# First layer of a two-layer network: VectorE makes the scaled input of the next tile between the driving term and the scan of this one

## The reference, cut to what matters

```python
Bm = sequence @ W_B.T + b_B
Cm = sequence @ W_C.T + b_C
Delta = softplus(sequence @ W_Delta.T + b_Delta + bias_Delta)
A_bar = exp(A * Delta[..., None])
B_bar = 1.0 / A * (A_bar - 1.0) * Bm[..., None, :]
...
state = state * Ab + x[..., None] * Bb      # one step of the scan over tokens
y = einsum('bdn,bn->bd', state, c)
...
x = layernorm(x + scan_layer(x))
x = layernorm(x + experts(x))               # silu(gate) * up, down, weighted by the router
```

## Time and profile before

| | |
|---|---|
| median of 3 runs | 3291.12 us |
| the profiled execution, its own time | 3293.81 us |
| its span (first to last instruction) | 3291.9 us |
| granted TensorE clock, mean | 0.97 |
| PE, busy share of the span | 91% |
| DVE | 80% |
| ACT | 68% |
| POOL | 68% |

### The profile page before, as it was taken

How to read it: one execution, slowest core, us unless ns; L and a number is a source line. 1 busy time by engine, 2 the same in 40 slices (tenths; PEclk the granted TensorE clock), 3 DMA queues, 4 the chain that set the end, 5 groups by cost and what they waited for, 6 DMA issues and landing times. The chain is left out here.

```text
span 3291.9 us, 40141 instructions
## 1 busy us (share of the span) xinstructions
PE 2997.8 (91%) x11488; PEld 1708.8 (52%) x11488; DVE 2647.5 (80%) x3505; ACT 2227.9 (68%) x3409; POOL 2244.2 (68%) x1623
## 2 busy tenths in 40 slices
PE   3589999999999999999889999999988899999998
PEld 1146666666666676778434434434434444444443
DVE  5989989898989899555799999999999545555553
ACT  2357676676767666666575666666665688888887
POOL 3478888888878788777477767777786444444444
PEclk7689999999999999999999999999999999999999
DMA  3024445444444444445222222222222333333332
GB/s 99 13 86 132 128 124 134 124 122 133 125 123 135 119 124 124 136 145 161 87 70 72 74 71 71 74 70 72 91 70 67 91 102 98 104 106 104 106 108 82
DMA packets 214983, 335.49 MB, mean 102 GB/s; under 512 B 36739, under 2 KB 72740, under 8 KB 214380
## 3 DMA queue, kind: packets, MB, share of 16 engines
q1 hardware_dynamic: 214764, 332.93, 35.3%
HBM read 325.69 MB, written 7.09 MB: 101 GB/s over the span
## 5 line engine op out<-in xcount | busy, mean ns | idle before, releaser
L1702 POOL TENSOR_TENSOR c_hc<-c_h,c_c_rep 128x1024 f32<-128x1024 f32 x256 | 604.2, 2361 | 251.4 <-DVE c_h L1746 183.0
L1746 DVE TENSOR_TENSOR_SCAN c_h<-c_decay,c_carry,c_v_ps 128x512 f32<-128x512 f32 x512 | 654.6, 1351 | 1.3 <-issue 1.3
L2170 ACT ACTIVATE d_hmid<-d_up,n_b 128x1024 f32<-128x1024 f32 x512 | 532.2, 1119 | 89.4 <-PE d_up L2072 89.2
L1581 ACT ACTIVATE c_decay<-c_dt,c_a_cols 128x512 f32<-128x512 f32 x512 | 363.9, 722 | 334.3 <-DVE c_h L1746 332.8
L2210 POOL TENSOR_TENSOR d_acc<-d_acc,d_prod 128x512 f32<-128x512 f32 x240 | 310.1, 1311 | 394.4 <-DVE d_prod L2278 394.4
L1398 PE MATMUL c_y_ps<-c_hc,ident 128*128 128x512 f32 x1024 | 500.7, 612 | 46.6 <-POOL c_hc L1702 37.5
L687 POOL TENSOR_TENSOR ab_inner_low<-ab_inner,ab_inner_high 128x512 fp32r<-128x512 f32 x264 | 341.8, 1295 | 241.5 <-ACT ab_inner_high L570 240.2
L559 ACT ACTIVATE ab_gate_ps<-ab_gate_ps,ab_raw_d 128x512 f32<-128x512 f32 x264 | 174.6, 661 | 430.0 <-PE ab_gate_ps L414 429.9
L669 POOL TENSOR_TENSOR ab_hc<-ab_h,ab_c_rep 128x512 f32<-128x512 f32 x256 | 331.7, 1296 | 86.7 <-DVE ab_h L740 65.1
L1736 DVE TENSOR_TENSOR c_v_ps<-c_dtu,c_b_ps 128x512 f32<-128x512 f32 x512 | 346.6, 766 | 1.7 <-PE c_b_ps L1389 1.1
L675 POOL TENSOR_TENSOR ab_gu_low<-ab_raw_gu,ab_gu_high 128x512 fp32r<-128x512 f32 x264 | 341.3, 1293 | 4.4 <-ACT ab_gu_high L546 4.4
(11 more groups left out here) (312 smaller groups left out, 6412.0 us busy)
## 6 DMA issues: line engine op xcount, KB each, us to landing
ab_raw_gu<-in_b_experts SPq DMA_DIRECT2D x264, 256.0 KB, 3.4
ab_w_rep<-ab_w_scratch SPq DMA_DIRECT2D x264, 256.0 KB, 3.6
c_c_rep<-c_c_scratch SPq DMA_DIRECT2D x256, 256.0 KB, 3.1
d_w_rep<-d_w_scratch SPq DMA_DIRECT2D x1024, 64.0 KB, 2.1
ab_raw_d<-in_b_experts SPq DMA_DIRECT2D x264, 129.0 KB, 2.1
ab_raw_x<-in_xT SPq DMA_DIRECT2D x32, 256.0 KB, 4.8
out<-xT SPq DMA_DIRECT2D x8, 512.0 KB, 3.0
xT<-in_xT SPq DMA_DIRECT2D x1, 3072.0 KB, 13.2
```

What stands on the lines that cost most here:

```text
L1581: nc.scalar.activation(decay[:, i % DEC, :], dt[:, s, m, :], ACT.Exp, scale=a_cols[:, n * NM + m:n * NM + m + 1]).then_inc(decay_ready, 1)
L1702: nc.gpsimd.tensor_tensor(hc[:, q % HC], h[:, q % HR], c_rep[:, q % BC].unsqueeze(1).broadcast_to([P, PAIR, CH]), ALU.mult).then_inc(hc_re ...
L1746: nc.vector.tensor_tensor_scan(out=h[:, q % HR, m, :], data0=decay[:, i % DEC, :], data1=v_ps[m][:], initial=carry[:, i:i + 1], op0=ALU.mu ...
L2170: nc.scalar.activation(hmid[:, (2 * q + r) % HM], up_ps[(2 * q + r + c * 2 * NU) % UP][:], ACT.Gelu, bias=b1[:, e:e + 1]).then_inc(gelu_re ...
```

## The change

The VectorE program of the first layer is written in another order. Inside a step the driving term of tile n comes first, then the scaled input of tile n + 1, then the scan of tile n. The scaled input of tile 0 of a chunk is made before the loop (first chunk) or at the end of step 32 of the iteration before. No instruction is added or removed, and no wait is added: each instruction keeps its own semaphore waits. Orders of all other engines are as before.

```diff
                     tile = n < NT and below(i, NCH)
                     if tile:
-                        scaled_input(i, s, n)
                         driving(i, n)
+                        if n + 1 < NT:
+                            scaled_input(i, s, n + 1)
                         scan(i, n)
                     if valid(g):
                         gated_input(g)
                         gate_times_up(i, n, g)
                         weigh(i, n, g)
+                    if n == NT and below(i, NCH - 1):
+                        scaled_input(i + 1, 1 - s, 0)
...
             dve.sem_inc(carry_ready, NT // NQ)
+            scaled_input(0, 0, 0)
             over_chunks(dve, NCH, lambda c, s, first, last: iteration(c, s))
```

## The result

The changed kernel takes 3306.88 us (median of 4 runs, 3305.0 to 3307.59); the kernel before, measured beside it, 3291.10 (4 runs, 3288.63 to 3291.36). The ratio is 1.0047, with a 95% interval of 1.0034 to 1.0060: slower by 15.8 us, where +4 was forecast. That is inside the range of 3282 to 3309, but outside the 3286 to 3302 of the forecast's own case. The execution that was profiled took 3305.0 us, its span is 3303.1; the profiled execution of before had 3293.81 and 3291.9.

What follows compares the result with a forecast made beforehand. With experts TensorE bounds the kernel, able to give back at most 8.1 of 180.5 us a stretch; without experts VectorE does. +2 with experts and +2 without, on 3291.1, made 3295 us; range 3282 to 3309.

Steps and rivals of the forecast that it cites:

- the forecast's own case: Whole kernel: the pairs of VectorE instructions close, handed back as waits for the replication; 3286 to 3302 us, chance 0.54.
- What an instruction costs by where it stands: VectorE: with independent successors the driving term takes 0.61 and the scaled input 0.65 us, saving 0.26 a tile, 8.2 a stretch.
- The nine waits: With experts, scaled inputs behind late TensorE gates wait for the replication at nine steps of 33, 12.3 us a stretch.
- The sum with experts: Stretch of 33 steps beside experts: 12.3 new waits less 8.2 saved less 3.8 vanished waits, +0.3 us; +2 over 6.3 stretches.
- the waits for the tanh: VectorE with experts: of 9.6 us a stretch spent waiting for ScalarE's tanh, 3.8 go.
- ten steps: Steps with experts counted beside six whole iterations, together 6.3 stretches at +0.3 us each.
- The first stage: The 55 tiles without experts: -0.9 us for regular tiles and +2.7 for late places, about +2.
- The tile at half clock: Without experts, scan end to scan end: 2.82 us at half clock where a tile took 2.71, and 2.52 at full clock.
- the clock's mix: First stage: mean clock 0.64 read as 72% half and 28% full, giving 2.2 - 3.1 = -0.9 us.
- the late places: First stage, replications behind projections and averages: 5.5 us, about half hidden beside VectorE's extra pieces, so +2.7.
- the replication in TensorE's queue decides: Rival: nine waits each 0.2 us longer, or first-stage late places paid fully at half clock; 3299 to 3312, chance 0.23.
- The prediction's bound: With experts, TensorE's unchanged work can give back at most 8.1 of 180.5 us a stretch, however fast VectorE becomes.

Runs made afterwards that it cites:

- experiment 9: The whole change plus three unread TensorE matmuls behind the replication of most tiles without experts, against the kernel before: 3298.99 us, ratio 1.0023.
- experiment 2: New VectorE order only in the 55 tiles without an expert, against the kernel before: 3301.82 us, ratio 1.0026.
- Experiments 3: New VectorE order only beside experts, and TensorE's replication in front of the gate instead of behind it, against the kernel before: 3283.22 us, ratio 0.9972.
- experiment 4: Old VectorE order, with TensorE's replication moved in front of the gate, against the kernel before: 3300.69 us, ratio 1.0025.
- 7: New VectorE order only beside experts, replication a step earlier behind the down matmuls of the step before, against the kernel before: 3291.95 us, ratio 1.0001.
- 8: Old VectorE order, replication a step earlier behind the down matmuls of the step before, against the kernel before: 3310.46 us, ratio 1.0056.
- 5: New VectorE order only beside experts, replication later, behind the six up matmuls, against the kernel before: 3434.29 us, ratio 1.0432.
- 6: Old VectorE order, replication later, behind the six up matmuls, against the kernel before: 3300.43 us, ratio 1.0026.
- Experiment 12: New VectorE order only beside experts, except for scaled inputs that belong behind the nine late gates, against the kernel before: 3299.96 us, ratio 1.0024.

## Why the prediction was right and wrong

**What an instruction costs by where it stands: right.** Where nothing holds it, the new scaled input starts 0.597 after the driving term (0.61 said) and the scan 0.664 after the scaled input (0.65 said), as means over the five stretches; the old pairs took 0.785 and 0.731. So 0.255 a tile is saved (0.26 said), 7.9 us a stretch (8.2 said), and the step on time takes 4.59 (4.62 said). The rule of the Trainium skill that was weighed, "VectorE: DVE Perf Modes", section "The DRAIN you can't avoid", by which nothing would be saved, is not what this trace shows. The same page, in "Two Vector instructions with no wait between them", says that a next instruction waits for all earlier ones to finish only if it is held; the 0.597 against a duration of 0.69 agrees with that.

**The nine waits: right in place, 0.1 us too short each.** They stand at steps 3, 6, 9, 15, 21, 23, 26, 27 and 30, as said, with one more of 0.2 at step 13. As the profile counts them they are 12.2 in the stretch shown (12.3 said) and 79.5 between 195 and 1400 us (75 to 85 said). But that count begins at the end of the driving term. Against 0.597 from start to start, the 31 intervals from driving term to scaled input, 31.8 us together, are 13.3 too long: at a place that waits, the overlap of 0.10 is lost as well.

**The sum with experts: +0.3 said, +0.94 measured.** By starts on VectorE: -7.9 saved, +13.3 waits for the replication, -4.5 from the scan to the gated input (the waits for the tanh; 3.8 said), -0.6 from the gated input to the next instruction, +0.5 at other instructions: 0.2 at the scaled and centred values, which now stand in front of a driving term, and 0.3 between two instructions of the router. That is +0.8, and +0.1 is spread over the rest. The term that was mis-sized is the wait (13.3, where 12.3 was said). Of the +0.94, 0.24 comes from one of the five stretches, the fourth iteration's, which took 182.64 (439.81 to 622.44) because TensorE's clock fell to half in it (last section); without it the loss is +0.70. From scan 54 to the third iteration's step 0, ten steps, the loss is another 2.3 us, against the 0.1 that they had as "ten steps" of a stretch. Most of it is one wait that the prediction did not have, at the switch to the stage with experts:

```profile
207.37 0.76 DVE L724 SCALAR_TENSOR_TENSOR ab_rep_ps<-ab_rep_ps,ab_inv_a,ab_b_rep 128x512 f32<-128x512 f32 x1 [4.68 <-PE ab_rep_ps L367]
```

Here the replication stands behind state sums, a projection that takes 3.78 us at half clock, and the first gate. Before, VectorE had a wait of 2.47 for the tanh at this place; the two steps take 11.9 us, where they took 10.2. With the clock up (experiment 9) they take 9.2. So from scan 54 to the eighth iteration the loss is 7 us where +2 was said.

**The first stage: the step that failed.** The tile at half clock took 2.83 (2.82 said) and 2.53 at full (2.52 said, seen in experiment 9). Two inputs of the sum failed. I put the clock's mix at 72% half, as before. With the change the mean clock fell to 0.56 (88% half), and experiment 2 has 0.57, while the traces with the old order in this stage have 0.59 to 0.65. By the prediction's own rule 88% would give +1.4; regular tiles cost +2.4 in the trace, instead of -0.9, because only 4 of 38 ran at the length of the full clock. And I took half of the 5.5 us of the late places as hidden beside VectorE's extra pieces. In the trace the sixteen other intervals cost a net +5.5, not +2.7: eight of them are 8.0 us longer together, eight are 2.5 shorter. Together +7.9 where +2 was said. Both were named in the rival, "the replication in TensorE's queue decides": late places in full, clock at half, a stretch that loses near 1 us, 3299 to 3312. That is the case that came, at 3307; I had given it 0.23, against 0.54 for the forecast. Its waits were to be 0.2 longer each; they were 0.1. So that 3307 lies in the stated range is owed to the rival, whose case the range took in, and not to the sum.

**What holds it all.** The prediction's bound was right: with experts TensorE's order sets the time. Experiments 3 and 4 show that the new order is worth 17.5 us once its replication is early (7 and 8 give 18.5, with the clock's part in it), and 5 and 6 that it costs 134 when it is late. Experiment 12 shows that removing the visible wait on VectorE alone brings nothing. What I did not foresee is that TensorE's own move costs 9 us (4, 6). With the old order a stretch then takes 182.1 to 182.2 instead of 180.7. In experiment 4 TensorE's idle time even shrinks, from 8.3 to 6.4 us a stretch, so its matmuls need 3.2 us more from start to start (waits too short to show beside the modelled ends can be part of that). At step 6 the gate starts 1.58 behind the end of the gated input instead of 1.00: the float32 average in front is now followed by the replication, and the 0.64 to the second start, which the gate's own first matmul had, now lies in front of the gate. How much of the 9 us that makes is not shown, and why the move behind up (6) costs as much as the one in front is open.

## What to carry to other kernels

An operation that is shortened by moving it earlier takes its input's deadline along: add up where its producer stands in its own engine's queue, and move the producer too, or the gain comes back as a wait. A wait that disappears from one engine and reappears on another with the same end was never the bound; leaving single late steps in the old order puts two of the moved pieces into the step behind, which here brought nothing. Where a sum leans on the mean clock of a stage, work out both levels and ask whether the change itself lets TensorE wait more there. And look at the switch between two stages by itself: its one long wait is in neither stage's average.

## What was unexpected of the hardware

In the stage with experts, which the mean gives as full clock, single drops occur. Three neighbouring windows of the changed kernel:

```profile
611.80:615.20 3.40, 1.24 (x6) 1.07 (x7) 1.94 (x3) 2.59 (x6) 1.46 (x2) 1.00 0.00 0
615.20:618.60 3.40, 3.40 (x10) 2.63 (x9) 2.14 (x5) 2.75 (x6) 3.40 (x4) 0.50 0.48 141
618.60:622.00 3.40, 3.40 (x16) 2.81 (x15) 3.04 (x5) 1.53 (x3) 2.82 (x3) 1.00 0.45 142
```

and what stands in them:

```profile
613.96 0.47 PE L414 MATMUL ab_gate_ps<-ab_xb_high,ab_gu_high 128*128 128x512 f32 x1 [2.26 <-DVE ab_tanh L755]
...
616.00 0.63 PE L426 MATMUL ab_up_ps<-ab_xb_high,ab_gu_high 128*128 128x512 f32 x1
616.43 0.63 PE L426 MATMUL ab_up_ps<-ab_xb_low,ab_gu_high 128*128 128x512 f32 x1
...
618.79 0.76 DVE L763 SCALAR_TENSOR_TENSOR ab_up_ps<-ab_up_ps,ab_raw_d,ab_tanh 128x512 f32<-128x512 f32 x1 [0.96 <-PE ab_up_ps L426]
```

After TensorE was idle for 2.26 us the granted clock is 0.50 for 3.4 us, although TensorE is busy all through that time; matmuls start 0.43 apart instead of 0.23, VectorE waits 0.96 for the product, and the stretch costs 1.2 us more. The same idle time at the same step of the four other iterations with this wait did not do it. A second drop of this trace, at 1393, came behind an idle time of 1.80 at another step. The kernel before has one between 198 and 1390 us (at 1249), behind 2.08. In the 14 traces together there are 34 such drops between 209 and 1400 us, up to four in one trace, and at each TensorE had just been idle for 1.5 to 2.7 us. So a kernel may win or lose some microseconds by it without a change of its order.

The second point is experiment 9: three extra matmuls a tile, which raise TensorE's busy time of the first stage from 84.6 to 110.7 of 160 us, bring the mean clock only from 0.56 to 0.73.
